# Scores of the self attention in two halves of the partitions, over two PSUM banks, in a fused perceiver layer

## The reference

```
x = x + cross_attention(layernorm(x), ctx, mask)   # 16 heads of 16, 257 context tokens, gated by a sigmoid
x = x + self_attention(layernorm(x))               # 16 query heads, 4 key/value heads of 16, causal, rotary, ternary weights
x = x + ffn(layernorm(x))                          # 8-bit activations, ternary weights, silu(z1) * z3, width 704
```

## Time and profile before

| what | value |
| --- | --- |
| median of the runs | 559.83 us (559.17 to 559.93, three runs) |
| the profiled execution | 561.7 us, its span 559.9 us from first to last instruction |
| granted clock of PE over the span | 0.999 |
| PE busy | 529.6 us (95%) |
| PEld busy | 434.8 us (78%) |
| DVE busy | 440.2 us (79%) |
| ACT busy | 416.2 us (74%) |
| POOL busy | 303.1 us (54%) |

### The profile page before, as it was taken

How to read it: one execution, slowest core, us unless ns; L and a number is a source line. 1 busy time by engine, 2 the same in 40 slices (tenths; PEclk the granted TensorE clock), 3 DMA queues, 4 the chain that set the end, 5 groups by cost and what they waited for, 6 DMA issues and landing times. The chain is left out here.

```text
span 559.9 us, 19727 instructions
## 1 busy us (share of the span) xinstructions
PE 529.6 (95%) x6876; PEld 434.8 (78%) x6876; DVE 440.2 (79%) x1389; ACT 416.2 (74%) x1147; POOL 303.1 (54%) x507
## 2 busy tenths in 40 slices
PE   8899999999999999999999999999999999999996
PEld 6677878787878778787877888787877878777775
DVE  2397775978879787988979797887979797889774
ACT  4897899887878787887877878887877788783221
POOL 4365756575573837375482847466483847243510
PEclk9999999999999999999999999999999999999999
DMA  8535221312123322313133332323233320100100
GB/s 247 187 97 184 77 71 48 109 47 91 43 72 86 76 86 71 87 33 100 53 73 87 80 87 62 92 44 83 59 74 87 107 67 4 59 21 8 31 12 9
DMA packets 42801, 42.16 MB, mean 75 GB/s; under 512 B 16080, under 2 KB 33488, under 8 KB 42704
## 3 DMA queue, kind: packets, MB, share of 16 engines
q1 hardware_dynamic: 42704, 40.90, 26.9%
HBM read 38.13 MB, written 2.75 MB: 73 GB/s over the span
## 5 line engine op out<-in xcount | busy, mean ns | idle before, releaser
L894 ACT ACTIVATE pr<-sm,nb 128x257 f32<-128x257 f32 x256 | 129.6, 509 | 24.7 <-DVE nb L1130 24.6
L1130 DVE CUSTOM_DVE_ANT_0 sm<-x_ps,mbias 128x257 f32<-128x257 f32 x256 | 99.5, 417 | 16.8 <-PE x_ps L1448 10.8
L671 POOL TENSOR_TENSOR cTl<-cx,cTh 128x512 fp32r<-128x512 f32 x64 | 84.3, 1325 | 35.8 <-ACT cTh L783 35.6
L783 ACT ACTIVATE pt<-x_ps 128x512 f32<-128x512 f32 x112 | 66.3, 595 | 12.7 <-PE x_ps L1458 12.4
L1458 PE MATMUL x_ps<-tab,pr 128*128 128x128 f32 x512 | 73.2, 275 | 0.4 <-DVE nb L1130 0.4
L1458 PEld LDWEIGHTS x_ps<-tab,pr 128*128 128x128 f32 x512 | 59.6, 141 | 9.3 <-issue 1.0
L677 POOL TENSOR_SCALAR rv<-mv 128x1 f32<-128x1 f32 x32 | 6.4, 200 | 100.5 <-DVE mv L994 91.8
L679 POOL TENSOR_TENSOR sr<-sv,halfneg 128x20 f32<-128x20 f32 x16 | 56.7, 3543 | 1.3
L1328 PE MATMUL x_ps<-wvTh,cTh 128*128 128x256 f32 x256 | 56.8, 303 | 0.0
L783 ACT ACTIVATE vv<-x_ps 128x512 f32<-128x512 f32 x64 | 38.0, 593 | 19.7 <-PE o_ps L1473 13.2
L1328 PE MATMUL x_ps<-wvTh,cTl 128*128 128x256 f32 x256 | 51.3, 282 | 0.0
(11 more groups left out here) (201 smaller groups left out, 1328.7 us busy)
## 6 DMA issues: line engine op xcount, KB each, us to landing
cx<-in_ctx SPq DMA_DIRECT2D x64, 256.0 KB, 4.1
mbias<-mask_bias SPq DMA_DIRECT2D x64, 128.5 KB, 3.5
xq<-in_x SPq DMA_DIRECT2D x16, 128.0 KB, 3.9
xr<-in_x SPq DMA_DIRECT2D x16, 128.0 KB, 3.7
vx<-end_values SPq DMA_DIRECT2D x64, 32.0 KB, 2.2
wraw<-self_values SPq DMA_DIRECT2D x64, 32.0 KB, 1.8
out<-yo SPq DMA_DIRECT2D x16, 128.0 KB, 1.9
fraw<-in_L_ffn_w SPq DMA_DIRECT2D x2, 704.0 KB, 6.7
```

What stands on the lines that cost most here:

```text
L671: g.tensor_tensor(cT[1][:, :, b % BT, :], cx[:, b % BT, :, :], cT[0][:, :, b % BT, :].bitcast(F32), ALU.subtract).then_inc(A_ctl, 1)
L783: return sc.activation(dst, src, ACT.Copy)
L894: sc.activation(pr[:, b % 2, gr, :], sm[:, b % 2, gr, :], ACT.Exp, bias=nb[:, n:n + 1], scale=-1.0, accum_out=st[:, 0, b, gr:gr + 1]).then ...
L1130: v.tensor_tensor_reduce(out=sm[:, b % 2, gr, :], in0=xb(f"S{b}", gr)[:, 0:LK], in1=mbias[:, b, :], scale=1.0, scalar=0.1 * NEG, op0=ALU.a ...
```

## The change

Queries and keys are laid out on all 128 partitions: the tokens of a tile are split in two halves, `s` = 0 for tokens 0 to 63 and `s` = 1 for tokens 64 to 127, and half `s` goes to partitions 64 s to 64 s + 63. The transposes become plain matmuls with 64 columns of the identity, 8 for the queries and 2 for the keys. `qTs` and `kbd` become 128 partitions x 256. The scores are again four matmuls, 64 partitions deep, but alternately on the lower and the upper half of the partitions, and the halves write to two banks: bank 0 for `s` = 0, bank 1 for `s` = 1. DVE adds the mask in two instructions of 128 x 256, each with its own count of `B_s2`. `SPARE` has other numbers (16: D_QT 8 to 10, D_kT 5 to 6, D_S 2 to 0, B_xT 7 to 9; 17: D_kT 12 to 13, D_S 7 to 5, C_xT 10 to 13). No step changes its place.

```diff
--- before.py
+++ after.py
@@ -58,7 +58,7 @@
 
 BANK = {
     "V1": (6,), "V2": (3,), "V3": (2,), "V4": (1,), "B_O": (0,), "B_oT": (3,), "B_wo": (5,), "B_xT": (5,),
-    "B_qkv": (5,), "D_QT": (1,), "D_kT": (3,), "D_S": (1,), "D_PV": (4,), "D_yT": (3,), "D_pj": (1,), "C_xT":
+    "B_qkv": (5,), "D_QT": (1,), "D_kT": (3,), "D_S": (0, 1,), "D_PV": (4,), "D_yT": (3,), "D_pj": (1,), "C_xT":
     (6,), "C_z0": (6,), "C_z1": (2,), "C_z2": (6,), "C_hT": (4,), "C_y": (4,), "GATE": (6,), "Q_h": (5,), "Q_q":
     (0,), "PT00": (3,), "PT01": (4,), "PT10": (4,), "PT11": (0,), "PT20": (4,), "PT21": (6,), "PT30": (5,),
     "PT31": (6,), "FS0": (0,), "TT0": (2,), "TT1": (0,), "TT2": (6,), "TT3": (6,), "FS1": (1,), "FS2": (0,),
@@ -306,11 +306,11 @@
 
 EARLY = 25
 SPARE = {
-    (16, "D_QT", 0): 8, (16, "D_kT", 0): 5, (16, "D_S", 0): 2, (16, "C_z", 0): 5, (16, "B_xT", 0): 7,
-    (16, "C_z", 2): 8, (16, "D_PV", 0): 24, (16, "D_yT", 0): 5, (16, "C_hT", 0): 15, (16, "C_y", 0): 4,
-    (17, "D_kT", 0): 12, (17, "D_S", 0): 7, (17, "C_xT", 0): 10, (17, "C_z", 0): 5, (17, "C_z", 2): 9,
-    (17, "D_PV", 0): 32, (17, "D_yT", 0): 5, (17, "C_hT", 0): 3, (17, "D_pj", 0): 2, (17, "C_y", 0): 1,
-    (18, "C_xT", 0): 37, (18, "C_z", 0): 5, (18, "C_z", 2): 9, (18, "C_hT", 0): 33, (18, "C_y", 0): 8,
+    (16, "D_QT", 0): 10, (16, "D_kT", 0): 6, (16, "C_z", 0): 5, (16, "B_xT", 0): 9, (16, "C_z", 2): 8,
+    (16, "D_PV", 0): 24, (16, "D_yT", 0): 5, (16, "C_hT", 0): 15, (16, "C_y", 0): 4, (17, "D_kT", 0): 13,
+    (17, "D_S", 0): 5, (17, "C_xT", 0): 13, (17, "C_z", 0): 5, (17, "C_z", 2): 9, (17, "D_PV", 0): 32,
+    (17, "D_yT", 0): 5, (17, "C_hT", 0): 3, (17, "D_pj", 0): 2, (17, "C_y", 0): 1, (18, "C_xT", 0): 37,
+    (18, "C_z", 0): 5, (18, "C_z", 2): 9, (18, "C_hT", 0): 33, (18, "C_y", 0): 8,
 }
 
 
@@ -351,7 +351,7 @@
         rows = tab[:, C_ROW:C_ROW + S]
         causal = tab[:, C_CAUS:C_CAUS + S]
         m4 = tab[:, C_M4:C_M4 + 4]
-        mj = tab[0:64, C_MJ:C_MJ + 4]
+        mj = tab[:, C_MJ:C_MJ + 4]
         cosT = tab[:, C_COS:C_COS + HD]
         sinT = tab[:, C_SIN:C_SIN + HD]
         ones = tab[:, C_ONE:C_ONE + P]
@@ -420,8 +420,8 @@
         ss, sv, sr, srg = sb("ss", [P, NQK]), sb("sv", [P, NQK]), sb("sr", [P, NQK]), sb("srg", [P, NQK])
         ra, rb, rc = (sb(n, [P, NQK, HD]) for n in ("ra", "rb", "rc"))
         rqk = sb("rqk", [P, NQK, HD])
-        qTs = sb("qTs", [64, BT, 4, S])
-        kbd = sb("kbd", [64, BT, KV, S])
+        qTs = sb("qTs", [P, 2, 4, S])
+        kbd = sb("kbd", [P, 2, KV, S])
         soft = sb("soft", [P, 5, BT * KV * S])
         s2, s3, p2, p3, p4 = (soft[:, n, :].rearrange("p (j k) -> p j k", k=S) for n in range(5))
 
@@ -494,7 +494,7 @@
         B_ss, B_sv, B_sr, B_srg = sig("B_ss"), sig("B_sv"), sig("B_sr"), sig("B_srg")
         B_ra, B_rb, B_rc, B_rr = sig("B_ra"), sig("B_rb"), sig("B_rc"), sig("B_rr")
         B_qTp, B_qTs, B_kTp, B_kbd = sig("B_qTp"), sig("B_qTs"), sig("B_kTp"), sig("B_kbd")
-        B_sp, B_s2, B_mx, B_s3, B_p2 = sig("B_sp"), sig("B_s2"), sig("B_mx"), sig("B_s3"), sig("B_p2")
+        B_sp, B_s2, B_mx, B_s3, B_p2 = sig("B_sp"), sig("B_s2", 2), sig("B_mx"), sig("B_s3"), sig("B_p2")
         B_dn, B_rc2, B_p3, B_p4 = sig("B_dn"), sig("B_rc2"), sig("B_p3"), sig("B_p4")
         B_pv, B_ys, B_yss, B_yv, B_yr = sig("B_pv"), sig("B_ys"), sig("B_yss"), sig("B_yv"), sig("B_yr")
         B_yTp, B_yTh, B_yTl, B_pp, B_x2 = sig("B_yTp"), sig("B_yTh"), sig("B_yTl"), sig("B_pp"), sig("B_x2")
@@ -511,13 +511,15 @@
         RELEASE = {
             "B_st": (B_o1, 1, -1, 1), "B_O": (B_o2, 1, -1, 1), "B_oT": (B_oTs, 1, -1, 1), "B_wo": (B_u1, 1, -1, 1),
             "B_xT": (B_xTl, 1, -1, 1), "B_qkv": (B_sq, 1, -1, 1), "D_QT": (B_qTs, 1, -2, 1), "D_kT": (B_kbd, 1, -2, 1),
-            "D_S": (B_s2, 1, -2, 1), "D_PV": (B_yss, 1, -2, 1), "D_yT": (B_yTl, 1, -2, 1), "D_pj": (B_x2, 1, -2, 1),
+            "D_PV": (B_yss, 1, -2, 1), "D_yT": (B_yTl, 1, -2, 1), "D_pj": (B_x2, 1, -2, 1),
             "C_xT": (C_xT, 1, -3, 1), "C_z0": (C_h, 3, -3, 1), "C_z1": (C_h, 3, -3, 2), "C_z2": (C_h, 3, -3, 3),
             "C_hT": (C_hT, 1, -3, 1), "C_y": (C_yo, 1, -3, 1), "GATE": (A_g, 1, 0, 1),
             "Q_h": (Q_hT, 1, 1, 1), "Q_q": (Q_qh, 1, 1, 1),
             "P_h": (Q_hT, 0, 0, 1), "P_q": (Q_qh, 0, 0, 1), "P_k0": (A_kh, 0, 0, 1), "P_k1": (A_kh, 0, 0, 2), "P_kx": (W_kx, 0, 0, 1),
             "P_v": (A_v, 0, 0, 1), "P_vx": (W_vx, 0, 0, 1),
         }
+        for n in range(2):
+            RELEASE["D_S", n] = (B_s2, 2, -2, n + 1)
         for n in range(4):
             RELEASE[f"TT{n}"] = (W_ev, 0, 0, 2 + n + 1)
         for n in range(3):
@@ -939,7 +941,7 @@
                         if due(i1 - 1):
                             act.wait_ge(B_sp, i1 - 1)
                         copy(qTs[:, :, :, :].rearrange("p b h q -> p h b q"),
-                             xb("D_QT")[0:64, :].rearrange("p (h b q) -> p h b q", h=4, b=BT)).then_inc(B_qTs, 1)
+                             xb("D_QT")[:, 0:D].rearrange("p (h b q) -> p h b q", h=4, b=2)).then_inc(B_qTs, 1)
                     elif k == "D_S":
                         act.wait_ge(B_s3, i1)
                         if due(i1 - 1):
@@ -1221,15 +1223,16 @@
                             dve.wait_ge(B_sp, i1 - 1)
 
                         v.tensor_tensor(kbd[:, :, :, :],
-                                        xb("D_kT")[0:64, 0:P].rearrange("p (b k) -> p b k", b=BT).unsqueeze(2).to_broadcast([64, BT, KV, S]),
-                                        mj.unsqueeze(1).unsqueeze(3).to_broadcast([64, BT, KV, S]), ALU.mult
+                                        xb("D_kT")[:, 0:2 * S].rearrange("p (b k) -> p b k", b=2).unsqueeze(2).to_broadcast([P, 2, KV, S]),
+                                        mj.unsqueeze(1).unsqueeze(3).to_broadcast([P, 2, KV, S]), ALU.mult
                                         ).then_inc(B_kbd, 1)
                     elif k == "D_S":
                         dve.wait_ge(B_sp, i1)
-                        v.tensor_tensor(s2[:, :, :], xb("D_S")[:, :].rearrange("p (j k) -> p j k", k=S),
-                                        causal.unsqueeze(1).to_broadcast([P, BT * KV, S]), ALU.add).then_inc(B_s2, 1)
+                        for n in range(2):
+                            v.tensor_tensor(s2[:, 8 * n:8 * (n + 1), :], xb("D_S", n)[:, 0:D].rearrange("p (j k) -> p j k", k=S),
+                                            causal.unsqueeze(1).to_broadcast([P, 8, S]), ALU.add).then_inc(B_s2, 1)
                     elif k == "D_mx":
-                        dve.wait_ge(B_s2, i1)
+                        dve.wait_ge(B_s2, 2 * i1)
                         v.tensor_reduce(mx2[:, :], s2[:, :, :], AX.X, ALU.max).then_inc(B_mx, 1)
                     elif k == "D_s3":
                         dve.wait_ge(B_mx, i1)
@@ -1540,21 +1543,28 @@
                         pe.wait_ge(was_read, n_read)
                         for h in range(4):
                             src = rqk[:, h * KV:(h + 1) * KV, :].rearrange("p j e -> p (j e)")
-                            last = tr(xb("D_QT")[0:64, h * P:(h + 1) * P], src, ident)
+                            for s in range(2):
+                                last = mm(xb("D_QT")[64 * s:64 * (s + 1), 64 * h:64 * (h + 1)], src, ident[:, 64 * s:64 * (s + 1)],
+                                          start=True, stop=True)
                         last.then_inc(B_qTp, 1)
                     elif k == "D_kT":
                         pe.wait_ge(B_rr, i1)
                         (was_read, n_read), = read("D_kT")
                         pe.wait_ge(was_read, n_read)
-                        tr(xb("D_kT")[0:64, 0:P], rqk[:, NH:NQK, :].rearrange("p j e -> p (j e)"), ident).then_inc(B_kTp, 1)
+                        for s in range(2):
+                            last = mm(xb("D_kT")[64 * s:64 * (s + 1), 0:64], rqk[:, NH:NQK, :].rearrange("p j e -> p (j e)"),
+                                      ident[:, 64 * s:64 * (s + 1)], start=True, stop=True)
+                        last.then_inc(B_kTp, 1)
                     elif k == "D_S":
                         pe.wait_ge(B_qTs, i1)
                         pe.wait_ge(B_kbd, i1)
-                        (was_read, n_read), = read("D_S")
-                        pe.wait_ge(was_read, n_read)
-                        for b in range(BT):
-                            last = mm(xb("D_S")[:, b * P:(b + 1) * P], qTs[:, b, :, :].rearrange("p h q -> p (h q)"),
-                                      kbd[:, b, :, :].rearrange("p j k -> p (j k)"), start=True, stop=True)
+                        for was_read, n_read in read("D_S"):
+                            pe.wait_ge(was_read, n_read)
+                        for b in range(2):
+                            for s in range(2):
+                                at = slice(64 * s, 64 * (s + 1))
+                                last = mm(xb("D_S", s)[:, b * P:(b + 1) * P], qTs[at, b, :, :].rearrange("p h q -> p (h q)"),
```

(3 more changed lines are left out.)

## The result

The changed kernel takes 567.71 us (median of four runs, 565.58 to 568.54), the kernel before 559.88 in the same session: a ratio of 1.0121, with an interval from 1.0069 to 1.0173. A second session gave 565.1 against 560.54, ratio 1.0079 [1.0047, 1.0111]. Both are slower than before by some 1%, and both times lie above the 560.7 us that was forecast and outside its range of 558.6 to 563.2. The profiled execution took 568.54 us, its span is 566.7.

A forecast was written before the change was run, and what follows sets the result against it. PE's stretch from D_QT to C_y, in a circle with DVE, was taken to bound each repeated tile. Terms -0.6 + 0.7 + 0.3 + 0.35 + 0.1 = +0.9 us on 559.83 gave 560.7 us, range 558.6 to 563.2.

The forecast's parts named there:

- The bound: Repeated tiles: PE's stretch from D_QT to C_y sets the length; what PE saves there shortens each of eleven tiles equally.
- The transposes: D_QT and D_kT on PE: ten rounds of two on two column halves, 0.70 us, so V ends 0.21 later.
- The scores: D_S on PE: eight records in four rounds of two, 0.64 us instead of 1.08, 0.44 shorter.
- the second rival: D_S on PE: halves don't run side by side, 1.08 us stays, +0.39 a tile; 567 us, chance 0.07.
- Piece 3: D_S needs bank 0, so waits until DVE reads piece 3 of S 0, at 293.25 instead of 293.50.
- The signal: From DVE's read of piece 3 to D_S's weight load, with a fourth wait: 0.12 to 0.23 us, taken as 0.17.
- The sign: Profile after: new PE wait before D_S at line 1130, some 0.2 us per repeated tile, over 1 in tile 14.
- The steady sum: Each repeated tile changes by -0.12 to +0.06 us, taken as -0.05; eleven tiles -0.6 us.
- Tile 14: DVE reads piece 3 of S 0 behind B_comb2, so D_S starts 1.16 later, less 0.44: +0.7 us.
- Tile 15: B_O on PE now waits for DVE's first half of the scores: +0.3 us, lower bound 0.1.
- The tail: Tile 16: B_wo ends 0.45 later, DVE takes it +0.28, mask halves +0.07, together +0.35 us; tile 17: +0.07.
- the third rival: Bank 0 waits cost more: both 0.23, kbd only 0.20 shorter, B_O late; 561.9 to 563.5 us, chance 0.2.

The follow-up runs named there:

- the variant with the moves: Changed kernel with DVE's B_o1 put behind piece 3 of S 0 in repeated tiles and piece 3 ahead of B_den in tile 14: 563.71 us, ratio 1.002.
- the experiment with three waits: Changed kernel without D_S's first wait where it repeats the bank 1 wait, three waits instead of four: 564.47 us, ratio 1.0077.
- fetches moved by 32: Changed kernel with 64 already met semaphore waits in PE's start-up, 32 more PE instructions in the trace: 563.78 us, ratio 1.0028.
- moved by 64: Changed kernel with 128 already met semaphore waits in PE's start-up, 64 more PE instructions in the trace: 568.75 us, ratio 1.0121.
- moved load: Changed kernel with a tile's second context load ahead of the first mask-bias load in SP's list: 564.0 us, ratio 1.0057.

## Why the prediction was wrong

By its steps, in quiet tiles, medians behind D_scale:

- **The bound.** Right for the quiet tiles. What PE does between D_scale and C_y sets the tile: 0.18 taken off D_S's start and 0.21 off B_O's took 0.20 off the tile (31.60 to 31.40), 0.16 off both took 0.15.
- **The transposes.** 16 and 4 records, V's first matmul at 0.79 behind D_scale against 0.55: V 0.24 later, forecast 0.21. They do run two by two.
- **The scores.** D_S from its load to S 1's: 0.67, forecast 0.64, which it takes where PE comes to it without a wait (0.645 in the variant with the moves); the second rival (1.08) is out.
- **Piece 3.** Its read ends 0.26 earlier, by `kbd`, as forecast (0.25), and D_S waits for it in every tile. The fourth wait is one more waiting instruction, as the forecast has it: before D_S the trace has 32 of them in the 16 tiles where it had 16. The signal took 0.23, the upper bound; I had taken 0.17, and the experiment with three waits gives 0.08. The sign that the forecast gave for it, a wait put down to the line of `nb` in each repeated tile, isn't there: in the groups by line and form it stands for 0.9 us, which is tile 14 alone, and in the repeated tiles the weight load's wait is put down to PE's own issue (0.3 us a tile):

```profile
L1566 PE MATMUL x_ps<-kbd,qTs 64*128 64x128 f32 x128 | 11.4, 294 | 2.6 <-DVE nb L1132 0.9 <-issue 0.2
```

- **The steady sum.** Forecast -0.05 a tile, -0.6 in all. Measured +0.03 at B_O in quiet tiles (the 0.06 of the signal and 0.03 of D_S, less 0.01 of `kbd`) and +0.01 in their length, and in three of the eleven, in the variant with the fetches moved by 32, 0.1 more (31.71 for 31.60; this starts at S 3, between two waits of PE, and its cause is open). Its eleven tiles take 0.28 less than those of the before that contains a long tile of 0.73, so 0.45 more without it: 1.05 off.
- **Tile 14.** +0.80 for +0.7; `kbd` at 455.11, piece 3 read at 456.89, D_S loaded at 457.12, which is the earlier trace rows in the new form:

```profile
455.11 0.41 DVE L1225 TENSOR_TENSOR kbd<-x_ps,tab 128x256 f32<-128x256 f32 x1
...
456.81 0.08 DVE L1132 DVE_READ_ACCUMULATOR2_ANT nb<- 128x1 f32 x1
457.12 0.55 PEld L1566 LDWEIGHTS x_ps<-kbd,qTs 64*128 64x128 f32 x8 [1.09 <-issue]
```

- **Tile 15.** B_O does stand behind the mask's first half now, to compare with the earlier trace rows:

```profile
488.12 0.75 DVE L1232 TENSOR_TENSOR soft<-x_ps,tab 128x256 f32<-128x256 f32 x2
488.59 0.20 PEld L1510 LDWEIGHTS x_ps<-tab,oT 128*128 128x128 f32 x2 [1.10 <-DVE soft L1232]
```

  B_O is 0.28 later behind D_scale, forecast 0.3. But the tile got 0.67 longer. 0.46 of it is again a transfer: DVE's update of x waits for the second load of x, 1.7 us of it (1.5 before), and this load is the eleventh in a row of transfers on SP, some of which wait for others. It landed 13.12 us behind D_scale before and 13.58 after; in the kernels moved by 64 and by 32 it landed at 13.13 and 14.21, and the tile took 31.20 and 32.28: 18.07 behind the landing each time, 17.85 before. So the change itself costs 0.22, and the row of transfers gives or takes up to 1 us. A fetch began at 2.9 us before, at 5.2 after, and at 3.4 and 5.1 in the kernels moved by 64 and by 32: the two late landings go with the two late fetches, but no run shows by itself that these are the reason.
- **The tail.** +0.46 for +0.35 in tile 16; DVE took B_wo's result 3.15 us behind D_scale's end instead of 2.91, +0.24 where I had 0.28, and the mask ended some 0.3 later. The 0.19 for the first change of mode (from column tiles to full weights) in that sum stands in no row, and no run shows it by itself. What the profile moved by 32 shows: the step behind D_QT starts 0.62 behind D_QT's first matmul instead of 0.46, the one behind D_kT 0.27 instead of 0.13, and B_wo 1.91 behind D_QT's first matmul (508.60 to 510.51) instead of 1.54 (507.80 to 509.34), +0.37 where the sum had 0.45. Tile 2: +0.19 in the first profile and 0.04 to 0.12 in the others, for 0.

With the long tiles away (moved load, or fetches moved by 32) the change costs 2.4 us of span at the full clock where the forecast had 0.9. In the profile with the fetches moved by 32 these are -0.28 in the eleven tiles, +0.11 in tile 2, +0.81 in tile 14, +1.31 in tile 15 and +0.46 in tile 16. Added to the 559.83 us of before this is a time of the third rival, which had 561.9 to 563.5 us, but only one of its three conditions came true: the signal cost its upper bound of 0.23, while `kbd` shrank by the full 0.26, and B_O was not held by DVE's half (0.62 from S 1's load to B_O's, as before).

The largest single part at the full clock is one that **no step of the forecast had**: it counted what the new instructions do, and not that they have to be brought in. Thirty-one more PE instructions a tile move the place of PE's code transfers from one tile to the next, and from a cycle of eight tiles with about one in the way of the loads (864 is 3 x 256 + 96) they came to one with every second tile at their edge (895 is 3 x 256 + 127): 1.95 us of the 4.35 at the full clock, 0.5 to 3.1 by execution. The step that failed is "a tile thus changes by ...; eleven tiles -0.6 us": the eleven took 2.71 us more in the first profile. It took eleven tiles alike, after the earlier trace rows of one, and put the transfer of the new instructions at nothing. The trace of before had one tile of 32.32, and the forecast calls the eleven alike.

In the first session the clock of the start-up came on top: three of the four runs of the changed kernel had a mean clock below 0.999, and of the four of before one took 563.47 us, a time of such runs. The late loads and the clock are each enough to leave the range: the one full-clock run of that session took 565.58 us, and with the load moved the full-clock runs have a median of 562.53 us, inside the range, and the six others take 563.95 us and more. The part of the clock is no effect that I can ascribe to the change; the same code ran at both levels, and 28 of the 78 later runs of before did it too. Whether the changed kernel does it more often (12 of 18 runs; the variant moved by 32 had 3 of 12) stays open. So 2.01 of the 6.8 us in the first profile are the luck of that execution. Open also is why a packet that begins at 5.5 to 6.2 delays the loads by more than the 0.96 us that it takes.

## What to carry to other kernels

Where a long unrolled program runs transfers with little slack, count the instructions that a change adds (31 a tile here), and look where the code transfers fall: one long tile among equal ones in the profile is a sign (32.32 us among ten of 31.6), and a load issued earlier than it need be was the cheap cure here (1.95 us of span). When a buffer gets a second owner, price the wait by the order on the engine that frees it: here one vector step put behind the read was worth 0.2 us a tile, as much as the wider layout gives with it (31.59 to 31.40), and 1.0 in tile 14. One waiting instruction less on a tensor engine that had nothing queued was worth 0.16 us here, and nothing where its own work was queued (D_S at 2.402 us in both): say each condition once.

## What the runs showed of the hardware that I had not expected

- Queue q8 (kind "instruction") moved 58 packets of 16,384 bytes between 18.1 and 549.8 us of the changed kernel's span, 0.96 us each (median; 0.96 to 1.08 by profile). They go with PE's instructions: 254 to 256 of these lie between two of them on average in all fourteen profiles, and with 32 more in the start-up of the changed kernel the fetches of the odd tiles began at -0.2 to 0.5 us, and no longer at 1.4 to 6.8. Where one began at 5.5 to 6.2 us behind D_scale, among loads of 256 and 128 KB, the load issued at 2.4 to 2.8 landed at 8.0 to 8.7 us instead of 6.4 to 7.1 (12 and 73 tiles of nine profiles).
- Two waits shared one PE instruction where 64 of them stood in a row: 32 instructions more in the trace (20281 for 20249), and 64 more for 128 waits (20313). Before D_S three waits are one waiting instruction and a wait that the first weight load itself has (line 1554, 16 in 16 tiles), four are two and the load (line 1562, 32). 31 such instructions between short matmuls cost 0.04 us each, one right behind a signal 0.16 us; in the start-up of the kernel before 32 of them cost nothing that can be told (ratio 1.0002), and where 64 stood PE was held up for 3.0 us.
- Eight records of 64 rows and 128 columns, alternately on two halves, take 0.67 us from the first load to the next step's (D_S, the tile of the earlier trace rows in its new form), against 1.08 on one half; ten pairs of 64-column records on two column halves put V 0.24 later than five transposes (0.79 behind D_scale against 0.55).
- The mean granted clock was lower in a third of the runs of one and the same kernel; in the profiles that show it, PE is at the lower level for 3.4 to 10.2 us of the start-up (6.8 in the first of the changed kernel, 10.2 in the second, which has 3.4 more in tile 14), and the median span of such runs is 3.3 us longer for the kernel before.
